# Two-layer cross-attention and expert kernel: the first 256 slots of layer 0's expert 0 are fetched before the last batch is routed, and multiplied between the last steps of the attention

## The reference, cut to what matters

```python
# B, S, D = 16, 112, 256 (1792 tokens); context of 375 keys; E = 8 experts, F = 1024
x = x + cross_attention_16_heads(layernorm(x), ctx) @ wo          # layer 0, attention
t = layernorm(x).reshape(1792, 256)                               # layer 0, experts:
logits = t @ wr.T                                                 #   top 2 of 8 experts,
vals, idx = top_k(logits, 2); gating = softmax(vals)              #   gates from a softmax
pos = cumsum(token chooses e) - 1                                 #   slot in expert e,
keep = pos < 560                                                  #   in the order of the tokens
y_e = gelu(xg_e @ w1_e + b1_e) @ w2_e + b2_e                      #   xg_e: the (<= 560) rows of e
x = x + sum over e of gate * y_e, added back to the tokens
x = x + one_head_attention(layernorm(x), ctx)                     # layer 1, attention
x = x + sum of 2 experts of w * ((silu(t @ w1_e) * (t @ w3_e)) @ w2_e)   # layer 1, experts
```

## Time and profile before

| what | value |
|---|---|
| median of three runs | 1029.47 us (1028.96 to 1030.52) |
| the profiled execution: its own time | 1030.73 us |
| its span in the trace | 1028.8 us |
| mean granted clock of TensorE | 0.936 of full |
| busy: PE, PEld | 915.5 us (89%), 846.5 us (82%) |
| busy: DVE, ACT, POOL | 694.9 us (68%), 437.5 us (43%), 469.9 us (46%) |
| longest single group | PE L351, the matmuls of the experts, 43% of the chain that ended last |

### The profile page before, as it was taken

How to read it: one execution, slowest core, us unless ns; L and a number is a source line. 1 busy time by engine, 2 the same in 40 slices (tenths; PEclk the granted TensorE clock), 3 DMA queues, 4 the chain that set the end, 5 groups by cost and what they waited for, 6 DMA issues and landing times.

```text
span 1028.8 us, 22198 instructions
## 1 busy us (share of the span) xinstructions
PE 915.5 (89%) x7911; PEld 846.5 (82%) x7911; DVE 694.9 (68%) x1982; ACT 437.5 (43%) x922; POOL 469.9 (46%) x440
## 2 busy tenths in 40 slices
PE   4799999899999749999999659855999999999997
PEld 3688988789888638999999637645999999999886
DVE  6567667477668447777776548875677787777443
ACT  3255545455554335666555324412333433333220
POOL 4124134241521436777666613653446545545514
PEclk9599999899999859999999879966999999999999
DMA  7797899887975167778877576636244336334102
GB/s 190 163 223 175 218 215 238 218 184 197 229 174 129 40 194 195 185 189 216 210 181 184 130 189 189 195 103 244 73 120 122 95 114 157 98 93 121 22 4 24
DMA packets 111824, 160.42 MB, mean 156 GB/s; under 512 B 12624, under 2 KB 100016, under 8 KB 109776
## 3 DMA queue, kind: packets, MB, share of 16 engines
q1 hardware_dynamic: 97760, 140.40, 51.3%
q0 software_dynamic: 13936, 18.33, 8.9%
HBM read 103.45 MB, written 56.96 MB: 156 GB/s over the span
## 4 chain that ended last, share of the span: by engine, by line
PE 50%; DVE 6%; DMA 3%; issue 3%; POOL 2%; ACT 1%; POOLq 0%; SPq 0%; DVEq 0%
PE ps L351 43%; PE ps L562 2%; DVE HTH L1421 2%; PE ps L650 1%; DMA x_scratch<-XG 1%; DMA XG<-xg_scratch 1%; POOL xg_scratch L1625 1%; PE ps L667 1%; PE ps L718 1%; DVE XN L1228 1%; DMA xg_scratch<-XN,dest 1%; DVE r_sel L1020 1%; PE ps L365 1%; DMA X<-x_scratch 0%; DVE st L1222 0%
## 5 line engine op out<-in xcount | busy, mean ns | idle before, releaser
L351 PE MATMUL ps<-XGH,WH 128*128 128x280 f32 (+1 forms) x768 | 220.1, 287 | 3.1 <-DVE GT L1417 2.2
L351 PE MATMUL ps<-XGL,WH 128*128 128x280 f32 (+1 forms) x768 | 221.5, 288 | 0.0
L351 PE MATMUL ps<-XGH,WL 128*128 128x280 f32 (+1 forms) x768 | 221.1, 288 | 0.0
L1681 POOL TENSOR_TENSOR HTL<-GT,HTH 128x280 fp32r<-128x280 f32 x112 | 115.0, 1030 | 163.9 <-DVE HTH L1421 163.9
L1275 DVE CUSTOM_DVE_ANT_0 NS<-ps,negm 112x375 f32<-112x375 f32 x256 | 135.4, 541 | 52.7 <-PE ps L457 52.5
L351 PE MATMUL ps<-WH,HTH 128*128 128x256 f32 (+1 forms) x536 | 153.0, 285 | 2.5 <-POOL HTL L1681 2.4
L351 PEld LDWEIGHTS ps<-XGH,WH 128*128 128x128 f32 x768 | 147.8, 192 | 4.0 <-DVE GT L1417 2.8
L351 PE MATMUL ps<-WL,HTH 128*128 128x256 f32 (+1 forms) x536 | 150.5, 281 | 0.0
L351 PE MATMUL ps<-WH,HTL 128*128 128x256 f32 (+1 forms) x536 | 150.2, 280 | 0.0
L351 PEld LDWEIGHTS ps<-XGH,WL 128*128 128x128 f32 x768 | 147.9, 193 | 0.0
L351 PEld LDWEIGHTS ps<-XGL,WH 128*128 128x128 f32 x768 | 147.5, 192 | 0.0
...
## 6 DMA issues: line engine op xcount, KB each, us to landing
...
```

Of the source, the lines that this page charges most:

```text
L351: m = e.matmul(out_ap, l, r, start=n == 0, stop=n == len(steps) - 1)
L1681: e.tensor_tensor(HTL[:, f, cols], GT[:, gi % NG, :], HTH[:, f, cols], ALU.subtract).then_inc(hl_pool[layer], 1)
```

## The change

Slots are given in the order of the tokens, so the first slots of an expert are filled by the first batches. The change uses this for expert 0 of both layers:

- The first 256 slots of expert 0 in layer 0 are to hold only tokens of batches 0 to 13. `shift` is how many of the 256 are still empty after batch 13 (none, where enough tokens chose the expert); batches 14 and 15 get slots that are moved on by it (`base1`). So these slots are complete when batch 13 is scattered.
- SP gathers them then (`first_rows_in`). TensorE transposes them at step (17, 5) and multiplies hidden units 0 and 1 at (17, 9), unit 2 at (17, 14) and units 3 to 7 at (18, 0), each engine with its part at the steps beside. When the experts start, row blocks 0 and 1 are multiplied at once, then the other three blocks are transposed.
- For this the groups of batches 12 to 15 are now 12 and 13, 14, and 15, with 14 steps (`tail_routes`) at (17, 8) and (17, 11), and the steps at which the counts are due are other ones.
- The halves of every expert are 256 and 304 columns (256 and 256 where it is narrow) and not 280 and 280 (232). The buffers of a half are tensors of their own.
- Weight chunks 1 to 3 are converted in batch 15's steps, chunk 4 behind the first two row blocks, chunks 5 to 9 beside the second half.
- In layer 1 the first 256 slots of expert 0 are gathered by themselves, and their hidden units are multiplied before the flags are read and the other blocks transposed; row blocks 0 and 1 stand ahead of the second half.
- At the end of layer 0's experts two weight chunks stand ahead of the last added row block rather than behind it, and the load of the second context moves behind the last row block.

The core of the diff (`turned` takes the place of TURNED; `pe_expert`, `act_expert`, `dve_expert` and `pool_expert` are the inner functions of the old expert functions, which the attention now calls too):

```diff
-HALF = 280
 RB = 128
+EARLY = 2 * RB
+HALVES = (EARLY, CAP - EARLY)
...
-CHUNKS0 = ((0, 4), (4, 4), (8, 4), (12, 3), (15, 1))
+
+CHUNKS0 = ((0, 4), (4, 4), (8, 4), (12, 2), (14, 1), (15, 1))
+LATE0 = 4
...
+        def turned(ex):
+
+            return {1: 0, 2: 2, 4: 4} if ex else {2: 0, 3: 2, 4: 4}
...
             if layer == 0 and ex == 0:
-                at = {(0, 1): 5, (0, 3): 6, (0, 5): 7, (1, 1): 8, (1, 3): 9}
+                at = {(1, 0): 5, (1, 1): 6, (1, 3): 7, (1, 4): 8, (1, 5): 9}
                 return at.get((hf, f))
+            if ex == 0:
+                return {(1, 3): 4 * E + 8, (1, 5): 4 * E + 9}.get((hf, f))
             n = (4 * ex if layer == 0 else 4 * E + 6 * ex) + 8 + hf
             return n if f == 3 and n < NCHUNK else None
 
+        def row_chunks(layer, ex, c):
+
+            base, per = (0, 4) if layer == 0 else (4 * E, 6)
+            if ex:
+                which = (c,) if c < per - 2 else ()
+            else:
+                which = {2: (0,), 3: (1,), 4: (2, 3)[0:per - 4]}[c] if c >= 2 else ()
+            return [n for n in (base + per * ex + 10 + i for i in which) if n < NCHUNK]
...
-            late = {3: H * (B + 1) + 7, 4: H * (B + 2) + 8}
+            late = {3: H * B + 9, 4: H * (B + 1) + 10, 5: H * (B + 2) + 8}
             at = {c: late.get(c, H * (b0 + nb + 2) + 11) for c, (b0, nb) in enumerate(CHUNKS0)}
             return next((c for c in at if at[c] + n == H * step[0] + step[1]), None)
+
+        def gate_due(step, n=0):
+
+            for c in range(len(CHUNKS0)):
+                if (H * (B + 1) + 9 == H * step[0] + step[1] - n) if c == 4 else counts_due(step, n + 1) == c:
+                    return c
+            return None
...
+        def pe_early_counts(e, layer, c):
+
+            bk = pe_bank(e, ("ec", layer), r_pg, pg_at(layer, c) + 1)
+            e.wait_ge(r_ms, layer * len(CHUNKS0) + c + 1)
+            e.matmul(ps[:, bk, 0:E], cst[0:S, C_ONE:C_ONE + 128], msum[:, c, :], start=True, stop=True).then_inc(full(bk), 1)
...
+                if (b, h) == (B + 1, 5):
+                    first_rows(0, 0)
+                if (b, h) == (B + 1, 9):
+                    first_unit(0, 0, 0, HALVES[0])
+                    first_unit(0, 0, 1, HALVES[0])
+                if (b, h) == (B + 1, 14):
+                    first_unit(0, 0, 2, HALVES[0])
+                if (b, h) == (B + 2, 0):
+                    for f in range(3, 8):
+                        first_unit(0, 0, f, HALVES[0])
+                c = counts_due((b, h))
+                if c is not None:
+                    route_counts(c)
+                    if c == LATE0 - 1:
+                        pe_early_counts(e, 0, c)
...
+            def unit(ex, hf, f, width):
+                if f == 0:
+                    e.wait_ge(xgl[layer], 3 * ex + (3 if hf else 1))
...
+            if layer == 1:
+                transposes(0, 0)
+                hidden(0, 0, HALVES[0])
+            e.wait_ge(r_fl, layer + 1)
             for ex in range(E):
-                if ex == 0:
-                    e.wait_ge(r_fl, layer + 1)
-                e.wait_ge(xgl[layer], 3 * ex + 2)
-                hidden(ex, 0, HALF)
-                e.wait_ge(xgl[layer], 3 * (ex + 1))
+                if ex:
+                    hidden(ex, 0, HALVES[0])
+                elif layer == 0:
+                    rows_out(0, 0, True)
+                    rows_out(0, 1, True)
+                    transposes(0, 2)
+                    transposes(0, 4)
+                else:
+                    transposes(0, 2)
+                    transposes(0, 4)
+                    rows_out(0, 0, True)
+                    rows_out(0, 1, True)
                 with e.If(e.value_load(fl[0:1, layer, ex:ex + 1], min_val=0, max_val=1)):
-                    hidden(ex, 1, HALF)
+                    hidden(ex, 1, HALVES[1])
                 with e.Else():
-                    hidden(ex, 1, NARROW - HALF)
-                for c in range(4):
-                    if ex + 1 < E and c in TURNED:
-                        transposes(ex + 1, TURNED[c])
+                    hidden(ex, 1, NARROW - EARLY)
+                for c in range(0 if ex else 2, 4):
+                    if ex + 1 < E and c in turned(ex):
+                        transposes(ex + 1, turned(ex)[c])
...
+                if b == B - 1 and h in (1, 3, 5):
+                    act_weights_hi(e, (h + 1) // 2)
+                if (b, h) == (B + 1, 6):
+                    first_hi(0, 0)
+                if (b, h) == (B + 1, 10):
+                    activated(0)
+                    activated(1)
+                if (b, h) == (B + 1, 15):
+                    activated(2)
+                if (b, h) == (B + 2, 1):
+                    for gi in range(3, 8):
+                        activated(gi)
...
+            if layer == 0 and c == LATE0 - 1:
+                bk = ready(e, ("ec", layer))
+                e.wait_ge(rv, Chain.at)
+                e.tensor_tensor(shift[:], cst[:, C_EARLY:C_EARLY + E], ps[:, bk, 0:E], ALU.subtract).then_inc(r_pg, 1)
+                yield
+                e.wait_ge(r_pg, pg_at(layer, c) + 1)
+                dve_ts(e, shift[:], shift[:], 0.0, None, ALU.max)
+                yield
+                dve_tt(e, base1[:], shift[0:S], cst[0:S, C_CAP:C_CAP + E], ALU.add)
+                marks["base1", layer] = Chain.at
...
+            tail_routes = {(B + 1, 8): 14, (B + 1, 11): 14, (B + 2, 4): 16, (B + 2, 10): 20}
...
-                advance(routes, 2 if n < N + H else 0 if (b, h) in ((B + 1, 5), (B + 1, 6), (B + 1, 9)) else 4 if n < N + H + 8 else 12,
-                        n >= N + H)
-                if b == B + 1 and h == 9:
+                if b == B - 1 and h in (4, 6):
+                    dve_weights_lo(e, h // 2 - 1)
+                if (b, h) == (B + 1, 7):
+                    first_lo(0, 0)
+                advance(routes, tail_routes.get((b, h), 2 if b < B else 4 if b == B else 0), b > B)
+                if (b, h) == (B + 1, 9):
+                    halves(0)
                     dve_normed(e, 2 + (b - 2) % 2, b - 2, rs2, b - 1, xn2)
+                if (b, h) == (B + 1, 12):
+                    halves(1)
+                if (b, h) == (B + 2, 1):
+                    halves(2)
+                if (b, h) == (B + 2, 5):
+                    for gi in (3, 4, 5):
+                        halves(gi)
             while routes:
                 advance(routes, 1, True)
-
-        def dve_experts(e, layer, between=None):
-            base, per = (0, 4) if layer == 0 else (4 * E, 6)
+            for gi in (6, 7):
+                halves(gi)
...
+            if layer == 1:
+                gathered_lo(0, 0)
+                for gi in range(8):
+                    halves(gi)
             for ex in range(E):
                 for hf in range(2):
+                    if ex == 0 and hf == 0:
+                        if layer == 1:
+                            gathered_lo(0, 2)
+                            gathered_lo(0, 4)
+                        rows_done(0, 0)
+                        rows_done(0, 1)
+                        if layer == 0:
+                            lo(4)
+                            gathered_lo(0, 2)
+                            gathered_lo(0, 4)
+                        continue
...
+                if b == B - 1 and h == 8:
+                    pool_weights_lo(e, 3)
+                if b == B and h in (12, 13):
+                    pool_scatter(e, 0, h)
+                if (b, h) == (B + 1, 11):
+                    pool_scatter(e, 0, B - 2)
+                if b == B + 2 and h in (1, 3, 5):
+                    halves_lo(h + 2)
+                if (b, h) == (B + 2, 10):
+                    pool_scatter(e, 0, B - 1)
...
+            for i in range(8):
+                e.wait_ge(d_sc[i], 16 * (4 if i < 4 else 3))
+            e.wait_ge(pr_done, 12 * (B - 1))
+            first_rows_in(e, 0)
+            for ex in range(2):
+                bias_in(e, ex)
             kept(B - 4)
-            for n in range(NSTG, NSTG + NR0):
+            for n in range(NSTG, NSTG + 4):
                 sp_chunk(e, n)
...
+        def first_rows_in(e, layer):
+
+            XG = ebufs[layer][0]
+            src = (xg_d, xg2_d)[layer].ap()[0:EARLY, :]
+            e.dma_start(XG[:, 0, 0:2, :], src.rearrange("(c p) d -> p c d", p=RB)).then_inc(d_xg[0], 16)
+
+        def bias_in(e, ex):
+            e.dma_start(B2[:, ex % 2, :], b2[ex:ex + 1, :].broadcast_to([128, D])).then_inc(d_b2, 16)
...
-                pieces = ((0, 4, d_xg[u]), (4, 5, d_xg[u])) if ex else ((0, 2, d_xg[0]), (2, 4, d_xg_first[0]), (4, 5, d_xg_first[1]))
+                pieces = ((0, 4, d_xg[u]), (4, 5, d_xg[u])) if ex else ((2, 4, d_xg_first[0]), (4, 5, d_xg_first[1]))
...
-                    context_t(e, 1)
...
+            context_t(e, 1)
```

255 lines of the change are left out of this document (146 added, 109 removed).

## The result

The changed kernel takes 1051.57 us (median of four; 1048.24 to 1055.43) against 1029.22 before (now with a fourth run): 1.0225 times the time before, with a 95% interval of 1.0199 to 1.0250. It is slower, as forecast, but by 22 us and not by 8, above the forecast range of 1027 to 1044.

The account below looks back on a forecast made before the run. TensorE was taken to bound the expert stage, with a serial chain in the hole ahead of it. Terms 6.7 + 1.7 + 3.7 - 4.0 = +8.1 us gave a median of about 1037.5, range 1027 to 1044.

Parts of the forecast that it names:

- (6): Layer 0, expert 0's second half: VectorE is late next, 14.4 us to block 2, which starts at 409.2, 6.3 later.
- (9): Hidden matmuls of the narrow experts, both layers: halves of 256 + 256 instead of 280 + 232 columns save 4.0 us.
- (1): Batch 15's attention steps: converting weight chunks 1 to 3 there delays TensorE by 1.9 us.
- (8): Layer 1, first expert: row blocks directly behind the units whose halves they need cost a net 3.7 us.
- (2): Batch 16's steps: routing of batches 12 and 13 moved there, ahead of a transpose on VectorE, costs 1.5 us.
- (3): Tail: first rows gathered at 361.4; batch 15's residual queues behind them on VectorE until 366.8, 9.0 us later.
- (4): Tail: hidden units delay batch 15's routing to 373.0; last scatter's second half starts at 384.1, remaining rows gathered at 389.6.
- (5): Layer 0, expert 0: row blocks 0 and 1 start at 382.9, about 4.5 us at half clock; second half at 394.8.
- (7): End of layer 0: POOL's chunk ahead of the last adds and the moved context load cost 1.7 us.
- D: Rival, slower by more: chunk 9 late and the clock falling again, +13 to +16 us, 1042 to 1045; chance 0.11.

Follow-up runs that it names:

- Experiment 3: Changed kernel with nothing of expert 0 ahead of batch 15's own work in the tail: 1046.65 us, ratio 1.0192.
- Experiment 7: Changed kernel with weight chunks 4 to 7 converted before ScalarE gates row blocks 0 and 1, only 8 and 9 beside the second half: 1044.38 us, ratio 1.0146.
- experiment 11: Changed kernel with the two weight chunks at the end of layer 0 behind the last added row block again: 1052.73 us, ratio 1.0232.
- experiment 2: Changed kernel with layer 1's expert 0 in the old order, two of its weight chunks put back with it: 1044.57 us, ratio 1.0162.
- experiment 1: Kernel before the change with only the widths of the halves altered to 256 + 304 (256 + 256 where narrow): 1028.88 us, ratio 1.0013.
- Experiments 10: Changed kernel with tail order, chunks and layer 1 reworked, plus a wait holding expert 0's hidden units until its remaining rows are gathered: 1051.90 us, ratio 1.0198.
- Experiment 13: Changed kernel with batch 15 first, old orders in layer 1 and layer 0's end, row blocks 0 and 1 behind the second half, chunks moved: 1027.49 us, ratio 0.9987.

## Why the prediction was wrong in size

The direction was right, and so was the main mechanism: the queues in the tail, and VectorE and POOL late in front of block 2. The steps that failed are (6) and (9); (1) and (8) were priced too low.

- **(1), (2) The last two batches.** Together forecast at 3.4; the last products with the values end 4.4 later (355.95 against 351.57), though the changed kernel's trace came to the wait 1.5 us earlier than the trace of before to that projection (330.12 against 331.61). (1) was under-sized: 2.8 of waiting and, in this kernel's two traces, 1.4 to 2.5 of clock, not 1.9. (2) was over-sized: 0.6, not 1.5.
- **(3), (4), (5) The queues behind the gather.** Right, to 2 us in the residual and to 0.5 us in the scatter, the row blocks and the second half's start. Experiment 3 shows the cause: with nothing of expert 0 ahead of batch 15, its residual and its scatter are back in their old place. Some of this agreement is luck. The last of the four scatters starts at 357.97 and not at 355.9, and TensorE has the first rows at 363.55 and not at 361.4; the residual is 1.6 late; then batch 15's routing starts at 373.62 (forecast 373.0), since unit 2 ran at the full clock, and the last scatter is on time. Of the table loads two more are in the trace, six for four, and the one back to the exponential takes 1.28 (378.46) with the next activation right behind it (379.76), as (4) took it. The 4.5 us at half the clock in (5) had no row with them; the changed trace has some 3.4 from 382.91 on.
- **(6) What is late next.** This step failed. Its mechanism was right (VectorE and POOL, with three chunks ahead of the last half) and it named the late chunk 9, but put it into the upper bound alone. From the second half's first matmul to block 2 it takes 17.1 us, not 14.4, because the last activations wait on ScalarE behind chunk 9. Then block 2 runs at half the clock, 5.47 us: the prediction followed the clock in the hole and left it out behind this wait. These are 2.7 and 2.4 us; expert 0 ends 11.3 later, not 6.7. Nothing was priced for expert 1, which takes another 2.0: its first activations now stand behind chunks 10 and 11 (TensorE waits for one at 424.27), and the waits in it come to 1.0; where the other 1.0 comes from is open. Experiment 7 gives 7 to 9 us back by moving chunks alone.
- **(7)** The last addition lands 2.0 later in relation to the last matmul (1.7 forecast), but nothing of it reaches the experts of layer 1: experiment 11.
- **(8)** The mechanism was right (row blocks now follow directly on the halves they need), the size 5.9 in the trace and 6.5 in experiment 2 for 3.7. Again the clock: block 2 there takes 4.60 us, 1.8 more than in experiment 2.
- **(9)** Failed: -4.0 was read from three short stretches of one expert, and the 0.118 for 256 columns came from matmuls of the row blocks. The hidden ones step by 0.118 to 0.120 in the changed kernel and by 0.119 to 0.120 in experiment 1, and at 0.120 a pair saves nothing; the prediction had taken 0.0046. Measured: +0.6 in the traces and 1.3 (-0.1 to 2.9) alone. The prediction set against it the Trainium skill's formula for a lone matmul ("TensorE: Matmul & The Clock Gate", Back-to-back issue gap), by which the time is linear in the columns and nothing is saved. Experiment 1 bears that out for the split; for the size the measurement decides, 0.118 to 0.120 us at 256 columns where the formula would have an estimated 0.109.

In the profiled executions the misses are 4.6 us in expert 0 of layer 0, 2.0 in expert 1, -2.0 in (7), 2.2 in (8) and 4.6 in (9); 8.1 becomes 19.4. The rest to 22.3 lies between the profiled executions and the medians. Of the rivals D came nearest (chunk 9, and the clock), with a chance of 0.11; it had the causes of (6) for layer 0 alone, and its 1042 to 1045 is still 7 us short.

Experiments 10 and 13 say where the expected gain went: about 8 us are won in the hole, and of these kernels only the one in which the queues in the tail, the chunks, the filler and layer 1 are all put right no longer gives them back. Experiment 13 undoes several things at once, so how much the filler has of it is not shown.
